# Expert routing and scatter moved inside an attention, a re-laid expert loop, and a gather joined with the following norm

## The reference, cut to what matters

```python
scores = x @ Wg + bg                      # (tokens, 8)
top1 = argmax(scores)
h = relu(x @ W1[top1] + b1[top1])         # 128 -> 512
out = h @ W2[top1] + b2[top1]             # 512 -> 128
```

## Time and profile before

| | us |
|---|---|
| median of 3 runs (range) | 2646.67 (2643.68 to 2651.2) |
| the profiled execution | 2642.58 |
| its span, first to last instruction | 2640.7 |
| TensorE's mean granted clock | 0.883 of full |
| stretch: layer norm 3 | 1126 to 1166 |
| stretch: ALiBi attention | 1166 to 1436 |
| stretch: experts, three Blocks | 1436 to 1679 |
| stretch: weights and layer norm 4 | 1679 to 1726 |

### The profile page before, as it was taken

One profiled execution on the slowest core, in us unless ns is written; L12 is line 12 of the kernel. 1 busy time (PEld: TensorE's weight loads), 2 busy tenths in 40 slices (PEclk: granted clock), 3 DMA queues, 4 the chain that ended last, 5 costly groups with the idle time before them and its releaser, 6 DMA issues. The chain is left out here.

```text
span 2640.7 us, 64964 instructions
## 1 busy us (share of the span) xinstructions
PE 2082.6 (79%) x25979; PEld 1309.1 (50%) x25980; DVE 1475.2 (56%) x3594; ACT 1136.0 (43%) x1852; POOL 720.8 (27%) x751
## 2 busy tenths in 40 slices
PE   4486999968699995946888185459987767999997
PEld 1132677743267763414555064236653324777774
DVE  5545788644578854346774132257772265666663
ACT  4542566643266654234665021316564430333333
POOL 0303676510466641021100402422110112122110
PEclk8787999989799998967999598569998865999999
DMA  3000000000000000004442401123430003333330
GB/s 122 0 0 0 2 3 3 3 1 0 0 3 3 3 3 1 0 22 116 102 105 62 166 0 52 39 70 97 97 82 1 36 16 104 107 116 102 104 100 33
DMA packets 92636, 124.12 MB, mean 47 GB/s; under 512 B 9328, under 2 KB 78448, under 8 KB 89008
## 3 DMA queue, kind: packets, MB, share of 16 engines
q1 hardware_dynamic: 90312, 116.00, 15.6%
q0 software_dynamic: 2048, 4.20, 0.5%
HBM read 69.83 MB, written 49.15 MB: 45 GB/s over the span
## 5 line engine op out<-in xcount | busy, mean ns | idle before, releaser
L1296 ACT ACTIVATE at_pr<-ps 128x768 f32<-128x768 f32 x256 | 198.6, 811 | 96.4 <-PE ps L1200 96.2
L1596 ACT ACTIVATE at_pr<-ps 128x768 f32<-128x768 f32 x128 | 103.8, 811 | 233.4 <-PE ps L1532 233.4
L697 POOL TENSOR_TENSOR la_tc<-la_ta,la_tb 128x512 f32<-128x512 f32 x128 | 162.8, 1272 | 114.2 <-DVE la_tb L993 110.3
L714 PE MATMUL ps<-w_l0f,la_hs 128*128 128x512 f32 x256 | 155.8, 693 | 45.1 <-DVE la_tb L993 38.6
L1340 DVE TENSOR_REDUCE at_m<-ps 128x2 f32<-128x512 f32 x256 | 174.6, 682 | 0.0
L1885 POOL TENSOR_TENSOR at_parts<-at_ta,at_tb 128x512 f32<-128x512 f32 x64 | 81.4, 1273 | 295.0 <-DVE at_tb L1875 295.0
L1339 DVE TENSOR_REDUCE at_m<-ps 128x2 f32<-128x256 f32 x256 | 108.6, 424 | 95.2 <-PE ps L1200 90.0
L684 POOL TENSOR_TENSOR la_qn<-la_tc,la_rn 128x512 f32<-128x512 f32 x128 | 134.2, 1048 | 52.8 <-issue 36.8
L1200 PE MATMUL ps<-cast 64*64 64x256 bf16 x2048 | 147.5, 277 | 0.0
L991 DVE TENSOR_TENSOR la_ta<-ps,la_tab 128x512 f32<-128x512 f32 x128 | 88.2, 689 | 97.6 <-ACT la_sq L917 97.6
L1514 PE MATMUL ps<-at_ks,at_qs 40*128 40x128 f32 (+1 forms) x1024 | 128.6, 373 | 13.6 <-DVE at_m L1639 7.1
(11 more groups left out here) (333 smaller groups left out, 5090.1 us busy)
## 6 DMA issues: line engine op xcount, KB each, us to landing
scratch_latent<-at_parts SPq DMA_DIRECT2D x32, 640.0 KB, 4.9
at_qs<-scratch_latent SPq DMA_DIRECT2D x32, 320.0 KB
at_ks<-scratch_latent SPq DMA_DIRECT2D x32, 320.0 KB
scratch_alibi<-at_parts SPq DMA_DIRECT2D x32, 192.0 KB, 2.4
at_ks<-scratch_alibi SPq DMA_DIRECT2D x32, 192.0 KB
scratch_rope<-at_parts SPq DMA_DIRECT2D x32, 192.0 KB, 2.2
at_ks<-scratch_rope SPq DMA_DIRECT2D x32, 192.0 KB
moe_weights<-in_moe SPq DMA_DIRECT2D x1, 4096.0 KB, 21.0
```

The costliest lines, as they stand in the source:

```text
L697: nc.gpsimd.tensor_tensor(tc[:, x, :], ta[:, x % 2, :], tb[:, x % 2, :], ALU.add).then_inc(s.la_tc, 1)
L714: nc.tensor.matmul(ps[:, 0, :], hs[:, i % QSLOTS, t * P:(t + 1) * P], w("wq" if p < 2 else "wk"), start=True, stop=True).then_inc(s.la_pro ...
L1296: nc.scalar.activation(pr[:, p % RING, :, :], ps[:, at:at + 2, 0:384], ACT.Exp, scale=scale).then_inc(s.at_prob, 1)
L1596: nc.scalar.activation(pr[:, p % RING, :, :], ps[:, 6:8, 0:384], ACT.Exp, scale=scale).then_inc(s.at_prob, 1)
```

## The change

- **Routing.** The first Block of `experts` is gone. `routing` gives hooks that `quad_attention` calls: POOL's constants before its row loop, SP's clearing of `experts_in` before the rows, gate scores and the turning of tiles 0 to 4 at the end of PE's and ACT's step 0, the rest in step 1, DVE's chain at the end of its steps 0 and 1, PE waiting for it at the end of step 2. The gate product now has the tokens as stationary operand, so scores come out by tokens: 32 products of 8 columns, no turning of scores. POOL scatters 3 chunks at the end of each of its steps from step 2 on (SCATTER is 2, EACH is 3), the last two in step 12. The table is cleared from a 128x128 tile of zeros, read 39 times.
- **SP.** It fills the ALiBi rows in step 2, behind the stores of rows 0 and 1; W2 and the biases (2576 KB) are loaded at the end of step 1, W1 (2048 KB) at the end of step 15, into Y, after all scatters.
- **Tiles.** All steps are written out. W1 is now stationary (four parts of 128 hidden channels) and the turned tile streams, so the hidden values come out by channels: the four turns per tile (L2121) are gone. POOL copies the expert's W1 (128x512) to a ring of three instead of the tile. One register read per tile on PE, DVE and POOL. The result is stored in three pieces of 23, 12 and 4 tiles.
- **Gather and norm.** `gathered_norm` is one Block: gathers wait by groups of 4, PE turns them, ACT applies silu while it copies out of PSUM, DVE does both gate steps, and the norm of tiles 0 to 3 runs before the turning of tiles 4 to 7. Layer 2's weights load beside the first gathers.

```diff
@@ quad_attention
             a.load_constant_rows(sp)
-            sp.wait_ge(s.at_zeroed, call + 1)
-            a.fill_constant_rows(sp)
             def step(i, n):
+                if i == 2:
+                    sp.wait_ge(s.at_zeroed, call + 1)
+                    a.fill_constant_rows(sp)
...
+                a.sp_side(sp, i)
...
+                if i == SCORE and x == 0:
+                    a.wait_constant_rows(pe)
...
+                a.pe_side(pe, i)     # and act_side, dve_side, pool_side, each at the end of step
@@ routing
+    FIRST, SECOND, SCATTER, EACH = 0, 1, 2, 3
...
+    def sp_first(sp):
+        sp.wait_ge(s.moe_init, 2)
+        sp.dma_start(g.by_tile(g.sorted_in, 0, XT), zero[:].unsqueeze(1).to_broadcast([P, XT, P])).then_inc(s.moe_cleared, 16)
+    def sp_step(sp, i, weights):
+        if i == 1:
+            sp.dma_start(k.w2b[:], weights[1]).then_inc(s.load_moe, 16)
+        if i == B - 1:
+            sp.wait_ge(s.moe_scattered, 16 * NCH)
+            sp.dma_start(k.Y[:], weights[0]).then_inc(s.load_moe, 16)
+    def pool_step(pool, i):
+        if i == SCATTER:
+            pool.wait_ge(s.moe_place, 1)
+            pool.wait_ge(s.moe_tokens, NT)
+            pool.wait_ge(s.moe_cleared, 16)
+        for c in range(EACH * (i - SCATTER), min(EACH * (i - SCATTER + 1), NCH)) if i >= SCATTER else ():
+            nc.gpsimd.indirect_dma_start(...)
+    def pe_step(pe, i):
+        if i == FIRST:
+            for c in range(NCH):
+                m = nc.tensor.matmul(ps[:, 2, c * NEXP:(c + 1) * NEXP], XN[:, c * P:(c + 1) * P], w("wg"),
+                                     start=(c == 0), stop=(c == NCH - 1), skip_group_check=True)
...
+        if i == SECOND + 1:
+            pe.wait_ge(s.moe_order, 10)
+            pe.wait_ge(s.moe_tokens, NT)
@@ experts, POOL and PE
+                for t in range(XT):
+                    e = chosen(pool, t)
+                    at_least(pool, s.moe_hidden, t - 2)
+                    nc.gpsimd.tensor_copy(w1[:, t % 3, :], W1[:, bass.ds(e * EH, EH)]).then_inc(s.moe_fetched, 1)
...
+                    if has(i, 1):
+                        t = i - 1
+                        e[t] = chosen(pe, t)
+                        pe.wait_ge(s.moe_features, t + 1)
+                        pe.wait_ge(s.moe_fetched, t + 1)
+                        at_least(pe, s.moe_biased, t - 1)
+                        for c in range(NHC):
+                            mm = nc.tensor.matmul(ps[:, 2 + t % 2, c * P:(c + 1) * P], w1[:, t % 3, c * P:(c + 1) * P],
+                                                  xT[:, t % 2, :], start=True, stop=True)
...
-                tile_pipeline(pe, step)
+                for i in range(XT + 3):
+                    step(i)
@@ gathered_norm, order of PE, ACT and DVE
+            for t in range(HALF):
+                turned(t)
+            products()
+            for i in range(HALF + 1):
+                if i < HALF:
+                    centre(i)
+                if i > 0:
+                    variance(i - 1)
+            for t in range(HALF, NT):
+                turned(t)
...
+            for half in range(2):          # ACT: swish, then square / rsqrt / square_root
+                for t in tiles:            # DVE: gated, then exact
+                    swish(t)
```

More of the change, by code:

```diff
@@ L1889, in latent_attention, with routing @@
     row_attention(k, 2, float(40.0 ** -0.5), 40, 5, PRODUCTS, (32, kvn), w("vd", rows=32), w("wo"), None, make)
-def experts(k, wgate, weights, both):
+def routing(k, w, sb):
     nc, s, ps = k.nc, k.s, k.ps
@@ new lines, in routing @@
+    hot = sb("hot", [P, NCH, NEXP])
+    io = sb("io", [P, NEXP])
+    zero = sb("zero", [P, P])
+    count_i = sb("counti", [P, XT], I32)
+    count = sb("count", [P, XT])
+    go_on = sb("goon", [P, NEXP, NCH])
+    total = sb("total", [P, NEXP, NCH])
+    upto = sb("upto", [P, NEXP, NCH])
+    more = sb("more", [P, NEXP, NCH])
+    tiles = sb("tiles", [P, NEXP])
+    end = sb("end", [P, NEXP])
+    begin = sb("begin", [P, NEXP])
+    ended = sb("ended", [1, XT, NEXP])
+    expert = sb("expert", [1, XT])
@@ new lines, in routing, with pool_first @@
+    g.sp_step = sp_step
+    def pool_first(pool):
+        nc.gpsimd.iota(count_i[:], [[1, XT]], base=0, channel_multiplier=0).then_inc(s.moe_iota, 1)
+        for e in range(NEXP):
+            m = nc.gpsimd.memset(io[:, e:e + 1], float(e))
+        m.then_inc(s.moe_iota, 1)
+        nc.gpsimd.memset(go_on[:], 1.0).then_inc(s.moe_init, 1)
+        nc.gpsimd.memset(zero[:], 0.0).then_inc(s.moe_init, 1)
+        pool.wait_ge(s.moe_init, 2)
+        nc.gpsimd.memset(go_on[:, :, 0:1], 0.0).then_inc(s.moe_iota, 1)
@@ new lines, in routing @@
+    g.pool_step = pool_step
+    def pe_step(pe, i):
[3 more added lines that the diff above has]
+                                     start=(c == 0), stop=(c == NCH - 1), skip_group_check=True)
+            m.then_inc(s.moe_scores, 1)
+        for t in (range(split) if i == FIRST else range(split, NT) if i == SECOND else ()):
+            at_least(pe, s.moe_tokens, t - RING + 1)
+            for q in range(4):
+                lo = t * TILE + q * P
+                m = nc.tensor.transpose(ps[:, 3 + t % RING, q * P:(q + 1) * P], XN[:, lo:lo + P], k.cf("identf"))
+            m.then_inc(s.moe_back, 1)
+        if i == SECOND:
+            pe.wait_ge(s.moe_hot, 5)
+            flat = hot[:].rearrange("p c e -> p (c e)")
+            n = NCH * NEXP
+            nc.tensor.matmul(ps[:, 2, 0:n], k.cf("mean"), flat, start=True, stop=True)
+            nc.tensor.matmul(ps[:, 2, n:2 * n], k.cf("before"), flat, start=True, stop=True
+                             ).then_inc(s.moe_prefix, 1)
+        if i == SECOND + 1:
+            pe.wait_ge(s.moe_order, 10)
+            pe.wait_ge(s.moe_tokens, NT)
@@ L1905, in experts @@
+    g.dve_step = dve_step
+    return g
+def experts(k, g):
+    nc, s, ps = k.nc, k.s, k.ps
+    XT = g.XT
+    NHC = EH // P
+    first = 4
+    cuts = [0, first, XT]
     sorted_out = nc.dram_tensor("experts_out", (XT * P, P), F32).ap()
-    by_tile = lambda dram, lo, hi: dram[lo * P:hi * P, :].rearrange("(t p) d -> p t d", p=P)
+    g.sorted_out = sorted_out
+    W1 = k.Y
+    W2, b2, b1 = (pack(k.w2b, W_MOEB[0])(name) for name in ("w2", "b2", "b1"))
     with ExitStack() as ctx:
         sb = lambda n, shape, dt=F32: ctx.enter_context(nc.sbuf_tensor(f"moe_{n}", shape, dt))
-        bias = sb("bias", [P, W_MOEB[1]])
-        wb = pack(bias, W_MOEB[0])
-        both_w = sb("weights", [P, W_MOE[1]])
-        w = pack(both_w, W_MOE[0])
@@ L1944, in _ @@
             def _(sp):
-                sp.wait_ge(s.moe_init, 2)
-                sp.dma_start(by_tile(sorted_in, 0, XT), ys[:]).then_inc(s.moe_cleared, 16)
-                sp.dma_start(both_w[:], weights).then_inc(s.load_moe, 16)
-                sp.dma_start(bias[:], both).then_inc(s.load_moe, 16)
-                sp.wait_ge(s.load_moe, 32)
+                sp.wait_ge(s.moe_scattered, 16 * g.NCH)
+                for j in range(2):
+                    sp.dma_start(xs[:, cuts[j]:cuts[j + 1], :], g.by_tile(g.sorted_in, cuts[j], cuts[j + 1])
+                                 ).then_inc(s.moe_sorted, 16)
+                    sp.wait_ge(s.moe_sorted, 16 * (j + 1))
@@ L1993, in _ @@
+                for i in range(XT + 3):
+                    step(i)
             @block.scalar
             def _(act):
-                for t in range(NT):
-                    act.wait_ge(s.moe_gate, t + 1)
-                    nc.scalar.activation(scores[:, t * TILE:(t + 1) * TILE], ps[0:NEXP, t, :], ACT.Identity,
-                                         bias=wgate("bg", rows=NEXP)).then_inc(s.moe_scored, 1)
-                for t in range(NT):
-                    act.wait_ge(s.moe_back, t + 1)
-                    nc.scalar.copy(tokens[:, t * TILE:(t + 1) * TILE], ps[:, 1 + t % 7, :]).then_inc(s.moe_tokens, 1)
@@ L2060, in experts @@
-        first = 4
-        cuts = [0, first, XT]
-        def tile_pipeline(eng, step):
-            last = first + (XT - first) // 2 * 2
-            for i in range(first):
-                step(i, i % 2)
-            with eng.Fori(first // 2, last // 2) as turn:
-                for n in range(2):
-                    step(turn * 2 + n, n)
-            for i in range(last, XT + 3):
-                step(i, i % 2)
-        def has(i, lag):
-            return not isinstance(i, int) or 0 <= i - lag < XT
@@ L2149, in step @@
+                def step(i):
                     if has(i, 0):
```

501 lines of the change are left out of this document (264 added, 237 removed).

## The result

The changed kernel takes 2557.3 us (median of four, 2550.7 to 2568.2) against 2648.8: ratio 0.9677, 95% interval 0.9640 to 0.9715. The forecast was 2520 in 2502 to 2550. The profiled execution has a span of 2548.9 us, 91.8 less than before, where 126.9 was forecast.

The account below looks back on a forecast made before the run. PE was taken to bound attention and tiles, POOL's indirect-DMA issuing the scatter and gather stretches. 66.5 + 35.0 + 32.9 - 7.5 = 126.9 us off 2642.58 gives 2515.7; plus 4.1 for the median, 2520 us, range 2502 to 2550.

Parts of the forecast that it names:

- Cost nothing: Attention rows: POOL's scatter issues, three a step at 1.27 us each, 40.6 us in all, were to add no time.
- Rows of more than 13.94 in the middle of attention: Sign named beforehand that the forecast is wrong: attention rows longer than 13.94 us, the row time before the change.
- Gather and norm, -32.9: Stage from first gather to norm's end: norm ends 18 us behind the last gather instead of 40.7, saving 32.9 us.
- my bound of -22: Gather and norm: the smallest saving allowed for, 22 us; the largest was 38.
- Rival 3: Gather and norm: DVE's in-order gate steps and the gathers' contention push the second half by 8 to 11 us: 2530; chance 0.06.
- First score, +3.5: Attention's start: transfers queued behind the clearing and W2 on SP put the first score at about 1201 instead of 1197.3.
- rival 2: SP's queue: big loads hold back stacks and maxima, or a start delay carries on: 25 us more, 2545; chance 0.14.
- W1's load, +4: Attention's end: W1's 2048 KB ahead of row 12's maxima make them 3 to 5 us late.
- Tiles, -35.0: Tiles stretch: PE steps of 2.1 us instead of 3.07, so 126.7 us become 91.7.
- Rival 1: Tiles: POOL's W1 copy and register read take 3.0 us and pace the tiles, 31 us more: 2551; chance 0.12.
- Rival 5: Attention: DVE locks POOL out while it writes descriptors; slower from 8.1 us a chunk, 2709 at 10; chance 0.03.
- Rival 4: Scatter not hidden: a late chunk makes SP's wait in step 15 hold up maxima and stack loads: 2550; chance 0.03.

## Why the prediction was right or wrong, step by step

In spans the first measurement is 35.1 us over the forecast: attention +32.6 (40.1 for 7.5), gather and norm +14.9, tiles -6.4 with their tail, unchanged work -6.0. The miss has two parts: 2557 against 2521 is the chip; 2521, at 0.9551 to 0.9562, against a forecast ratio of 2519.8/2646.7 = 0.9521 is the sum's own error.

**"Cost nothing" for the scatters in the rows: the step that failed.** On chips 7, 8 and 9 it holds. In the first measurement ten rows took 158.9, against 138.3 on chip 9: 20.6 us, on chip 4 22.9. The term was put at nothing. I had costed what is queued behind POOL and asked only whether POOL comes late; it did not. The price was paid by DVE and ACT, which waited for TensorE's signals, 1.7 and 2.9 us late in the row end shown. "Rows of more than 13.94 in the middle of attention" was the sign I had named.

**Gather and norm, -32.9.** 30.9 on chip 9 (91.7 to 60.8), 18.0 in the first measurement, beyond my bound of -22. Same sign: the overlap is given back. That both stages have one cause is argued from their going together. Rival 3 had the direction (8 to 11 us late; 14.9 came) and half the path: DVE's gate steps of the second half stand behind the first half's norm in its order, and ended 61.4 us after the first gather, where the sum had 47 and chip 9 shows 47.3. What made them late was not the gathers' contention but TensorE's signals in the first half.

**First score, +3.5.** It was +14.3 to +17.0 (45.5 and 48.2 against 31.2). The steps that were wrong: the routing's first share on PE, allowed 14 us and set against 20 us of cover, took 17.8 (13.66 for the gate products alone) between products 0 and 1, and pushed row 1's parts, on which SP waits with everything behind it. And the fill, moved to step 2, I did not count at all: every instruction moved past SP's queue counts, and this one stood in the way. Moving fill and load gave back 13.2 us of the score on chip 4 (47.4 to 34.2); the first cast gained less, 7.4 (58.1 to 50.7): it now comes 16.5 us behind the first score, in the kernel before 9.9, since W2's load stands ahead of row 1's stacks. This is rival 2 in kind.

**W1's load, +4.** Right: +6.0 and +6.1 for the five rows, 4.6 to 4.9 of it gone when it is moved.

**Tiles, -35.0.** Better: -39.8 on chip 9, -40.9 in the first measurement. PE steps after the change, and POOL's copies of weights:

```profile
1539.98 1.06 PE L2128 MATMUL ps<-moe_xt,moe_w 128*128 128x128 f32 x8
1540.88 0.27 PE L2134 MATMUL ps<-conf,moe_xs 128*128 128x128 f32 x1
1540.99 1.06 PE L2140 MATMUL ps<-w_moe,moe_ht 128*128 x8
1541.88 1.06 PE L2128 MATMUL ps<-moe_xt,moe_w 128*128 128x128 f32 x8
```

```profile
1539.31 0.61 POOL L2112 COPY moe_w<-y 128x512 f32 x1 [1.28 <-PE ps L2128]
1541.21 0.61 POOL L2112 COPY moe_w<-y 128x512 f32 x1 [1.28 <-PE ps L2128]
```

A step takes 1.90 us with no gap, not 2.1: the written-out step before still held 0.15 that went with the new order; of what, the rows don't tell. Rival 1 falls: POOL waits 1.28 for PE each time.

**Rival 5** had engines block each other over POOL's descriptors, but the other way round: POOL kept its 0.97, DVE waited. The Trainium skill, page SBUF — State Buffer, section SBUF: two separate sides, says that on SBUF's ports PE, ACT and DVE's own pair never wait on anyone. The rows do not speak against it: a square still takes 0.60; what is late is TensorE's signal ahead of it, and why stays open.

**Rival 4** (a late chunk holds up SP) did not occur: in the changed kernel on chip 9 SP issued W1's load right behind its stores in step 15.

## What to carry to other kernels

That work is only issued, and off the path, does not make it free for the others; where it runs beside a full engine, compare an instruction's start with its releaser's end. An in-order DMA queue is costed with every transfer that is moved past it, the small fills too, and a big load belongs behind the last small transfer that someone waits for soon. Before explaining a surprise, run the unchanged kernel beside the experiment, and once on another chip: a stage that the edit does not touch is the control.

## What the runs showed of the hardware

The executions are of two kinds for this program. In one kind (chip 4 and the first measurement, which may be the same chip), TensorE's signals come late while POOL issues indirect DMAs and for some us after: 1.7 and 2.9 us in the row end shown, 2.4 (ahead of the fold copies) to 9.9 us (ahead of the second square) in the norm; VectorE and ScalarE wait for them. In the other (chips 7, 8, 9) the signals come 0.01 to 0.03 us after the matmul's modelled end in the same places, and the engines start at once. Clock (0.88 against 0.89 over the attention), POOL's pace (0.97 an issue) and the length of the others' instructions are the same. The changed kernel takes 35 us (1.4%) more in the first kind; the kernel before, which issues its indirect DMAs beside idle engines, takes 6 to 11 more (0.2 to 0.4%), and in its traces 3.3 us of such a difference lie in a row without an indirect DMA. Whether it is the chip or a lasting state of it, whether the indirection, the software queue or the bytes set it off, and why TensorE's signals are late, stays open: the runs that would tell fell on quick chips.
